# Layer-norm moments of x: sums from a ninth column of the gate products, squares on ScalarE

## The reference

```python
Q = h @ Wq.T; K = h @ Wk.T                      # h = ctx_512, four heads, added up
sim = einsum(Q, K) / (sqrt(32) * 4)             # [4, 512, 512]
mask = sim >= (153rd largest of the row)
A = sigmoid(sim) * mask; A = (A + A.T) / 2
x = x + tanh(g_xattn) * ((1 - gamma) * layernorm(x) + gamma * A)
xn = layernorm(x)
scores = xn @ gate_w.T                          # 8 experts
w, idx = top_k(softmax(scores), 2); w = w / w.sum()
x = x + tanh(g_ffn) * sum_a w_a * w2[idx_a] @ (silu(w1[idx_a] @ xn) * (w3[idx_a] @ xn))
```

## Time and profile before

| | us |
|---|---|
| median of 3 runs (lowest, highest) | 819.46 (818.11, 819.76) |
| the profiled execution, its own time | 819.61 |
| its span | 818.0 |
| TensorE busy | 732.3 (90%) |
| VectorE busy | 397.1 (49%) |
| ScalarE busy | 286.4 (35%) |
| GpSimd busy | 147.7 (18%) |
| VectorE's BN_STATS of x (L813), 16 of them | 9.9 |
| GpSimd's scaling of x (L411), 16 instructions | 12.1 |
| TensorE's base products (L483), 128 records | 27.45 |

### The profile page before, as it was taken

How to read it: one execution, slowest core, us unless ns; L and a number is a source line. 1 busy time by engine, 2 the same in 40 slices (tenths; PEclk the granted TensorE clock), 3 DMA queues, 4 the chain that set the end, 5 groups by cost and what they waited for, 6 DMA issues and landing times.

```text
span 818.0 us, 10944 instructions
## 1 busy us (share of the span) xinstructions
PE 732.3 (90%) x3390; PEld 592.0 (72%) x3391; DVE 397.1 (49%) x930; ACT 286.4 (35%) x475; POOL 147.7 (18%) x199
## 2 busy tenths in 40 slices
PE   7393099378999999999999999999999999999996
PEld 3193077356888888888888888888888888888885
DVE  3888977742256222822265238223652372365222
ACT  4854657430144111611253126111621351162111
POOL 2271004770101001101001011010011110001110
PEclk9755598577999999999999999999999999999998
DMA  8842034556514611182115512821264227221111
GB/s 309 328 155 103 13 144 188 203 194 243 156 26 128 245 39 26 26 334 39 39 32 202 177 26 31 328 39 39 39 238 134 35 44 306 52 39 26 26 30 22
DMA packets 23727, 98.18 MB, mean 120 GB/s; under 512 B 2784, under 2 KB 3040, under 8 KB 19872
## 3 DMA queue, kind: packets, MB, share of 16 engines
q0 software_dynamic: 10992, 66.21, 26.4%
q1 hardware_dynamic: 12576, 31.81, 11.4%
q10 hardware_dynamic: 144, 0.00, 0.0%
HBM read 73.72 MB, written 24.30 MB: 120 GB/s over the span
## 4 chain that ended last, share of the span: by engine, by line
issue 71%; DVE 9%; PE 7%; POOL 6%; POOLq 3%; DVEq 1%; DMA 1%; ACT 0%; SPq 0%
POOL out L435 4%; PE bank L516 2%; POOL routed L400 2%; DVE front L855 2%; PE bank L507 2%; POOLq L256 1%; PE bank L505 1%; POOLq L434 1%; PE bank L467 1%; DVE top L953 1%; DVE ln_stats L813 1%; DVE front L950 1%; DVE rows_own L830 1%; POOL raw L443 1%; PE bank L457 1%
## 5 line engine op out<-in xcount | busy, mean ns | idle before, releaser
L549 PE MATMUL bank<-w_hi,xT_hi 128*128 128x512 f32 x560 | 225.9, 403 | 2.9 <-DVE xT_lo L1119 2.9
L550 PE MATMUL bank<-w_hi,xT_lo 128*128 128x512 f32 x560 | 222.5, 397 | 0.0
L551 PE MATMUL bank<-w_lo,xT_hi 128*128 128x512 f32 x560 | 222.0, 396 | 0.0
L757 ACT ACTIVATE act_g<-bank 128x512 f32<-128x512 f32 x70 | 41.7, 595 | 330.6 <-PE bank L551 328.2
L549 PEld LDWEIGHTS bank<-w_hi,xT_hi 128*128 128x128 f32 x560 | 105.9, 189 | 27.1 <-issue 3.3
L551 PEld LDWEIGHTS bank<-w_lo,xT_hi 128*128 128x128 f32 x560 | 105.8, 189 | 25.8
L550 PEld LDWEIGHTS bank<-w_hi,xT_lo 128*128 128x128 f32 x560 | 106.0, 189 | 23.6
L549 PE MATMUL bank<-w_hi,hT_hi 128*128 128x512 f32 x280 | 116.2, 415 | 0.0
L1135 DVE TENSOR_TENSOR hT_lo<-bank,hT_hi 128x512 fp32r<-128x512 f32 x70 | 48.4, 692 | 137.5 <-ACT hT_hi L761 137.5
L1013 DVE TENSOR_TENSOR w_lo<-raw,w_hi 128x1024 fp32r<-128x1024 f32 x88 | 104.4, 1222 | 20.1 <-ACT w_hi L673 18.4
L673 ACT ACTIVATE w_hi<-raw 128x1024 fp32r<-128x1024 f32 x88 | 91.4, 1059 | 60.0 <-PE bank L551 50.5
(11 more groups left out here) (192 smaller groups left out, 669.1 us busy)
## 6 DMA issues: line engine op xcount, KB each, us to landing
raw<-weights POOLq DMA_DIRECT2D x21, 2048.0 KB, 16.0
xtile<-routed SPq DMA_DIRECT2D x36, 260.5 KB
raw<-weights SPq DMA_DIRECT2D x3, 2048.0 KB, 7.8
xb<-x SPq DMA_DIRECT2D x4, 1024.0 KB, 11.0
raw<-xT SPq DMA_DIRECT2D x4, 1024.0 KB, 9.0
w_hi<-weights POOLq DMA_DIRECT2D x2, 2048.0 KB, 10.2
out<-xb SPq DMA_DIRECT2D x4, 1024.0 KB, 4.2
routed<-pad SPq DMA_DIRECT2D x8, 260.5 KB, 2.4
```

The costliest lines, as they stand in the source:

```text
L549: nc.tensor.matmul(out_ap, hi, hi_w, start=start, stop=False)
L550: nc.tensor.matmul(out_ap, lo, hi_w, start=False, stop=False)
L551: return nc.tensor.matmul(out_ap, hi, lo_w, start=False, stop=stop)
L757: nc.scalar.activation(act_g[:, s, :], bank[GATE[s]][:, :], ACT.Silu).then_inc(silu_set[s], 1)
```

## The change

VectorE takes no moments of x any more. `gate_c` gets a ninth column of ones, so each base product also gives the row's sum of x; `means(b)` (one VectorE instruction on four values per partition, read from PSUM) turns it into `minus_mean_x`. ScalarE's new `spreads_x(b)` squares x about that mean with an accumulator, four instructions per batch, and GpSimd's `base_scales(b)` waits for that. TensorE starts the base products of batch b only when `means(b - 1)` has read its sums. `gate_c` is made earlier, `xT` 0 and 1 are loaded ahead of x, the load of the third weight group waits for `spreads_x(3)` too, `sigmoids(1)` moves behind the masks' last count, and `base_score` moves from ahead of the thresholds to ahead of `x1(0)`.

```diff
         gate_w = sb("gate_w", [P, DC, E], F32, part1)
-        gate_c = sb("gate_c", [P, DC, E], F32, part1)
+        gate_c = sb("gate_c", [P, DC, E + 1], F32, part1)
...
-        ln_mv = sb("ln_mv", [P, B, TB, 2], F32, part1)
+        minus_mean_x = sb("minus_mean_x", [P, B, TB], F32, part1)
+        spread_x = sb("spread_x", [P, TILES], F32, part1)
...
+        squares_x = raw[:, 2, TILES * P:TILES * P + TB * N].rearrange("p (i n) -> p i n", n=N)
...
-        base_ps = bank[7][:, 256:256 + TILES * E].rearrange("p (t e) -> p t e", e=E)
+        base_ps = bank[7][:, 256:256 + TILES * (E + 1)].rearrange("p (t e) -> p t e", e=E + 1)
...
+
+            def load_xT(b):
+                sp.dma_start(xT_in_raw[b % 2], xT[b]).then_inc(xT_in[b], 16)
+
+            load_xT(0)
+            load_xT(1)
             for b in range(B):
                 sp.dma_start(xb[:, b, :, :], x_tiles[b]).then_inc(x_in[b], 16)
-
-            def load_xT(b):
-                sp.dma_start(xT_in_raw[b % 2], xT[b]).then_inc(xT_in[b], 16)
-
-            load_xT(0)
-            load_xT(1)
             sp.dma_start(raw[:, 0, :], w_groups[0, 0]).then_inc(raw_in_0[0], 16)
             for b in range(2, B):
                 sp.wait_ge(base_mm, b - 1)
@@ -285,6 +286,7 @@
             sp.wait_ge(base_mm, B)
             sp.dma_start(raw[:, 1, :], w_groups[0, 1]).then_inc(raw_in_0[1], 16)
             sp.wait_ge(all_counted, 1)
+            sp.wait_ge(spread_x_set, B)
             sp.dma_start(raw[:, 2, :], w_groups[0, 2]).then_inc(raw_in_0[2], 16)
...
+            nc.gpsimd.memset(gate_c[:, :, E], 1.0)
...
             def base_scales(b):
 
-                pool.wait_ge(ln1_stats, b + 1)
-                then(nc.gpsimd.tensor_scalar(ln_v[:, 0, b, :], ln_mv[:, b, :, 1], EPS, 1.0, ALU.add, ALU.mult))
+                pool.wait_ge(spread_x_set, b + 1)
+                then(nc.gpsimd.tensor_scalar(ln_v[:, 0, b, :], spread_x[:, TB * b:TB * (b + 1)], 1.0 / D, EPS, ALU.mult, ALU.add))
                 then(nc.gpsimd.tensor_tensor(ln_r[:, 0, b, :], ln_v[:, 0, b, :], rsqrt_pow[:, :], ALU.pow))
-                then(nc.gpsimd.tensor_tensor(ln_m[:, 0, b, :], ln_r[:, 0, b, :], ln_mv[:, b, :, 0], ALU.mult))
+                then(nc.gpsimd.tensor_tensor(ln_m[:, 0, b, :], ln_r[:, 0, b, :], minus_mean_x[:, b, :], ALU.mult))
                 nc.gpsimd.tensor_scalar(ln_s[:, b, :], ln_r[:, 0, b, :], c1, 1.0, ALU.mult, ALU.add)
-                nc.gpsimd.tensor_scalar(ln_o[:, 0, b, :], ln_m[:, 0, b, :], neg_c1, 1.0, ALU.mult, ALU.mult).then_inc(ln1_set, 1)
+                nc.gpsimd.tensor_scalar(ln_o[:, 0, b, :], ln_m[:, 0, b, :], c1, 1.0, ALU.mult, ALU.mult).then_inc(ln1_set, 1)
...
                 pe.wait_ge(xT_in[b], 16)
+                if b > 0:
+                    pe.wait_ge(mean_x_set, b)
                 for i in range(TB):
...
+            def spreads_x(b):
+
+
+                act.wait_ge(mean_x_set, b + 1)
+                act.wait_ge(x_in[b], 16)
+                if b > 0:
+                    act.wait_ge(spread_x_set, b)
+                for i in range(TB):
+                    t = TB * b + i
+                    last = nc.scalar.activation(squares_x[:, i, :], xb[:, b, i, :], ACT.Square, bias=minus_mean_x[:, b, i:i + 1],
+                                                scale=1.0, accum_out=spread_x[:, t:t + 1])
+                last.then_inc(spread_x_set, 1)
+
+            spreads_x(0)
             act.wait_ge(probe_final, 1)
             for t in range(TILES):
+                if t == TB or t == 2 * TB:
+                    spreads_x(t // TB)
                 if t == 3 * TB:
                     act.wait_ge(half_counted, 1)
                     sigmoids(0)
-                    sigmoids(1)
                 act.wait_ge(masked_set, t + 1)
                 last = count_masked(t)
                 if t == TILES // 2 - 1:
                     last.then_inc(half_counted, 1)
             last.then_inc(all_counted, 1)
+            sigmoids(1)
+            spreads_x(3)
...
-            def row_moments(b, tiles):
-                for i in tiles:
-                    V.bn_stats(ln_stats[:, i, :], xb[:, b, i, :])
-
-            def aggregate(b):
-                dve.drain()
-                for i in range(TB):
-                    last = V.bn_aggr(ln_mv[:, b, i, :], ln_stats[:, i, :])
-                last.then_inc(ln1_stats, 1)
-                dve.drain()
-
-            def x_stats(b):
-                dve.wait_ge(x_in[b], 16)
-                row_moments(b, range(TB))
-                aggregate(b)
+            def means(b):
+                dve.wait_ge(base_mm, b + 1)
+                V.tensor_scalar(minus_mean_x[:, b, :], base_ps[:, TB * b:TB * (b + 1), E], -1.0 / D, None, ALU.mult).then_inc(mean_x_set, 1)
...
-            V.tensor_scalar(c2, small[:, 1:2], 0.5, None, ALU.mult)
+            V.tensor_scalar(c2, small[:, 1:2], 0.5, None, ALU.mult).then_inc(gains_set, 1)
             dve.drain()
-            V.tensor_scalar(neg_c1, c1, -1.0, None, ALU.mult).then_inc(gains_set, 1)
...
             sim_spread(0)
-            dve.wait_ge(x_in[0], 16)
-            row_moments(0, range(2))
             first_probes(0)
             sim_rows(2)
             flag(0, 0)
             sim_rows(3)
             sim_spread(1)
-            row_moments(0, range(2, TB))
-            aggregate(0)
             first_probes(1)
+            dve.wait_ge(gate_sums, 1)
+            V.scalar_tensor_tensor(gate_c[:, :, 0:E], gate_ps.unsqueeze(1).to_broadcast([P, DC, E]), -1.0 / D,
+                                   gate_w[:, :, :], ALU.mult, ALU.add).then_inc(gate_set, 1)
             second_probes(0)
             flag(1, 0)
             second_probes(1)
-            x_stats(1)
-            dve.wait_ge(gate_sums, 1)
-            V.scalar_tensor_tensor(gate_c[:, :, :], gate_ps.unsqueeze(1).to_broadcast([P, DC, E]), -1.0 / D,
-                                   gate_w[:, :, :], ALU.mult, ALU.add).then_inc(gate_set, 1)
             for k in range(1, SEARCH):
                 for half in range(2):
                     flag(half, k)
                     next_probes(half, k)
-                    if k == 1:
-                        x_stats(2 + half)
+                    if k < 3:
+                        means(2 * (k - 1) + half)
...
                     V.max(top8[:, t, :], masked[t]).then_inc(top8_set, 1)
-            dve.wait_ge(base_mm, B)
-            dve.wait_ge(ln1_set, B)
-            V.tensor_tensor(base_score[:, :, :], base_ps, ln_s[:, :, :].rearrange("p b i -> p (b i)").unsqueeze(2).to_broadcast([P, TILES, E]),
-                            ALU.mult).then_inc(base_out, 1)
             dve.wait_ge(all_counted, 1)
...
+            def base_scores():
+                dve.wait_ge(ln1_set, B)
+                V.tensor_tensor(base_score[:, :, :], base_ps[:, :, 0:E], ln_s[:, :, :].rearrange("p b i -> p (b i)").unsqueeze(2).to_broadcast([P, TILES, E]),
+                                ALU.mult).then_inc(base_out, 1)
...
             mask_A(0)
             mask_A(1)
             first_low(0, range(1))
+            base_scores()
             x1(0)
             mask_A(2)
```

More of the change, by code:

```diff
@@ L107, in build @@
         gain_in = sb("gain_in", [P, 3], F32, part1)
-        gain = sb("gain", [P, 6], F32, part1)
-        tanh_x, gamma, tanh_f, c1, c2, neg_c1 = (gain[:, k:k + 1] for k in range(6))
+        gain = sb("gain", [P, 5], F32, part1)
+        tanh_x, gamma, tanh_f, c1, c2 = (gain[:, k:k + 1] for k in range(5))
         small = sb("small", [P, 16], F32, part1)
@@ L133, in build @@
         max8 = sb("max8", [P, 8], F32, part1)
-        ln_stats = sb("ln_stats", [P, TB, 6], F32, part1)
-        ln_mv = sb("ln_mv", [P, B, TB, 2], F32, part1)
+        minus_mean_x = sb("minus_mean_x", [P, B, TB], F32, part1)
+        spread_x = sb("spread_x", [P, TILES], F32, part1)
         ln_v = sb("ln_v", [P, 2, B, TB], F32, part1)
@@ L232, in build @@
         gains_act, gains_set = sem("gains_act"), sem("gains_set")
-        ln1_stats, base_set = sem("ln1_stats"), sem("base_set")
+        mean_x_set, spread_x_set, base_set = sem("mean_x_set"), sem("spread_x_set"), sem("base_set")
         ln1_set, ln2_set, pads_in = sem("ln1_set"), sem("ln2_set"), sem("pads_in")
@@ L272, in _ @@
             sp.dma_start(gate_w[:, :, :], gateT).then_inc(gate_in, 16)
-            for b in range(B):
-                sp.dma_start(xb[:, b, :, :], x_tiles[b]).then_inc(x_in[b], 16)
             def load_xT(b):
@@ L280, in _ @@
             load_xT(1)
+            for b in range(B):
+                sp.dma_start(xb[:, b, :, :], x_tiles[b]).then_inc(x_in[b], 16)
             sp.dma_start(raw[:, 0, :], w_groups[0, 0]).then_inc(raw_in_0[0], 16)
@@ L515, in even_scores @@
                     for c in range(DC):
-                        last = nc.tensor.matmul(scores_ps[b][:, i, :], even[b][:, c, i * P:(i + 1) * P], gate_c[:, c, :],
+                        last = nc.tensor.matmul(scores_ps[b][:, i, :], even[b][:, c, i * P:(i + 1) * P], gate_c[:, c, 0:E],
```

## The result

The changed kernel took 820.67 us (median of 12 runs, 819.68 to 821.50), the kernel before 819.28 us (12 runs, 817.67 to 820.16, on the same chip). The ratio is 1.0016, 95% interval 1.0008 to 1.0023. So the change costs about 1 us, some 0.1%, near the edge of what can be told from none. 820.9 us was forecast.

The account below looks back on a forecast made before the run. VectorE paces the front, up to the first scatter, ahead of TensorE's unchanged expert loop. Terms -1.0 + 1.6 + 0.8 = +1.4 us on 819.61 gave 821.0, 820.9 for a median; range 817.2 to 823.4.

Parts of the forecast that it names:

- The hand-over: Between TensorE and VectorE per batch: a cycle of 7.3 us against 4.2 us of VectorE work, stalls some 3.0 us.
- The search: VectorE's half rounds ahead of the masks: they end at 73.1 instead of 74.10 us, -1.0 us.
- The block of batch 0's scaling: GpSimd's L411 holds up three small steps of VectorE's last half round by 0.5 us each, 1.5 us.
- The masks: VectorE's mask groups: L411 of batches 1 and 2 delays L947s and small steps; +1.6 us, bounds 0 and 3.6.
- Batch 3: L411 over mask_A(1) and first_low delays x1(0), ScalarE's spreads and the first scatter: +0.8 us, bounds 0 and 1.5.
- Gentle sharing: Rival: VectorE's long mask instructions lose nothing beside L411; 818.7 us, chance 0.22.
- Harsh sharing: Rival: L411 meets the L947s fully, 1.7 us a batch, if batch 1's starts after 87.2; 823.3 us, chance 0.20.
- Half-length pieces of TensorE: Sign of base products at TensorE's full clock, where the three stalls vanish: 811.9 us, chance 0.08.

Follow-up runs that it names:

- late means: Changed kernel, but TensorE doesn't wait for the means between batches and VectorE takes all four after the last half round: 811.11 us, ratio 0.9894.
- the two banks: Changed kernel with base products of batches 1 and 3 in another PSUM bank, TensorE waiting for the mean before last: 821.33 us, ratio 1.0008.

## Why the prediction was right, point by point

- **The hand-over** was right in kind and size. The cycle is 7.31 us (TensorE's 49.95 to 57.26), forecast 7.3; the stalls are 3.15 us, forecast 3.0. The parts are 0.31 + 6.97 + 0.04 us, forecast 0.30 + 6.86 + 0.10. A piece is 6.97 us, not 6.86: the ninth column, costed at nothing, has at most 0.03 us a batch of that, since two batches run together take 13.79 us, 6.90 each, in the late means; the rest is the lone piece's end. The late means show the other side: without the wait the stalls and the block go, 10.5 us of the search (47.64 to 37.17), and with no scaling on either side what the stalls cost is 9.0 us (46.19 to 37.16).
- **The search** was forecast to give 1.0 us: 1.05. The block of batch 0's scaling was priced at 1.5 us; it is 1.33 us (5.53 less the 4.20 of a quiet half round), and 1.45 by the profile that leaves the scaling out. Against it stands a new gap of 0.3 us on VectorE in the first round (ahead of L890 at 33.88 us: 0.52 us idle), ended by nothing that the profile shows, in every kernel with the change. It was not priced, and its cause is open.
- **The masks** were forecast at +1.6 us and took 1.53, as the sum of other terms. The groups cost 0.52 and 0.81, 1.33 us, where 1.6 was priced; `base_score` gave its 0.19 here; and the idle time ahead of the memset at L989 is 1.62 us where it was 1.24, +0.38, again under "issue". The last was not foreseen: it holds in all changed kernels and stays open, since no kernel here moved it by itself. So the total came out right by two errors that cancel, 0.3 us too much for the groups against 0.38 us that was missing. The L954 instructions, which read two inputs, lost nothing in the changed kernel; GpSimd's small steps waited for them (1.10 us for one of 0.26), as the forecast said.
- **Batch 3** was the wrong term: +0.8 us forecast, 0 measured. The step that failed is the place of L414: "L411 then lies over `mask_A(1)` and `first_low`", which was to put x1(0) 1.6 us back. The small steps were taken at 2.39 us, their price in the search, though they ran beside the masks of two inputs; they took 5.1 us (106.35 to 111.42), one of them 1.34 us (L388 above). So L414 began as the eight masks ended, and met x1(0) instead. `minus_mean` starts 0.3 us and ends 0.7 us later than before against the first of the masks, and the 0.7 us between it and the spreads, which the prediction did count, take that up. The later part of the path, of which it said "I see no slack there", was never put to the test.
- **The rest of the total.** The front costs 0.5 us, the medians 0.7 to 1.4. In the profile the stretch from the first scatter to the end is 684.6, 683.3 and 683.1 us in the changed kernel, 684.7 and 682.7 in the one before, no difference that five values can show when two of the same kernel lie 2.0 us apart. What makes up the other 0.2 to 0.9 us of the medians is not settled; the stretch from the shares to the scatter, 1.15 us longer in one profile of three, could hold it, but no run shows that. The forecast 820.9 stood within 0.3 us of the first median in part by luck: it has a term of 0.8 us that is nothing, and the medians hold up to 0.9 us that the front doesn't show.
- **The rivals.** Gentle sharing fell with the mask groups of 2.18 and 2.47 us. Harsh sharing fell too: a group lost 0.5 and 0.8 us, not 1.7, and L414 of batch 1 started at 86.30, on the near side of the 87.2 given as its point. Half-length pieces of TensorE never came; the granted clock was 0.5.

The Trainium skill, "SBUF — State Buffer", "Who interferes with whom", says that whoever issues first holds the shared pair for its whole instruction and the other is blocked. The traces agree with that on both sides. In the late means L414 had begun (69.34 us) ahead of the second mask group, and the two-input L954 took 2.90 us instead of 2.50. In the changed kernel, where GpSimd came into a running string of them, only GpSimd lost.

## What to carry to other kernels

Taking 9 us of work off an engine gave nothing here, because each piece of it was replaced by a wait of the same length: before moving a sum to another engine, compare the pace of the producer with that of the consumer, and take the results where the consumer needs them, not where the old work stood. Here the means were needed only after the search, and taking four small instructions there, and TensorE's wait for them out, turned +1 us into -8.4. And a difference of 1 us between two profiles means little until each stretch is measured from its own start and a second profile of each kernel is there.

## What the runs showed that I had not expected

TensorE's pace doubles once near the start, at 10 to 13 us, and the moment differs from run to run. Its weight loads for the similarity products, in the changed kernel:

```profile
10.78 0.34 PEld L470 LDWEIGHTS bank<-front 128*128 128x128 f32 x1 [0.52 <-issue]
11.63 0.34 PEld L470 LDWEIGHTS bank<-front 128*128 128x128 f32 x1 [0.52 <-issue]
12.22 0.19 PEld L470 LDWEIGHTS bank<-front 128*128 128x128 f32 x1 [0.25 <-issue]
12.65 0.19 PEld L470 LDWEIGHTS bank<-front 128*128 128x128 f32 x1 [0.24 <-issue]
```

They stand 0.85 us apart, then 0.43, though the windows give a granted clock of 1.00 from 9 to 14 us. In the first profile of before the change of pace came some 1.7 us earlier, which at half the pace is the whole of the 0.88 us. What sets the moment is open.

A gain in the front can be taken back where TensorE's clock drops behind it. From the first shares to the first scatter it takes 6.27 or 6.28 us in five of the twelve profiles and 7.39 to 9.03 us in the other seven. In the five the granted clock is 1.00 in each of the last three windows of 4 us ahead of the shares; in the seven it is 0.50 to 0.75 in the last of them and 0.68 to 0.93 in the one before. The third profile of the changed kernel, one of the seven, in its last 4 us ahead of the shares:

```profile
123.66:127.66 4.00, 4.00 (x14) 2.29 (x13) 3.75 (x20) 2.38 (x8) 1.37 (x3) 0.73 0.56 219
```

The first two profiles of the same kernel have 1.00 there, so the program doesn't fix it alone. Nor does the moment alone: the kernel before began its masks after the thresholds at 104.95 us and kept the full clock, the third profile of the changed kernel at 105.24 us and did not. What decides it is open. In the profiled executions it took 1.6 of the 2.5 us that the kernel before gained without its scaling, and 2.7 us of the two banks, more than they had gained there.
